# Attention with the scores made transposed: 128 keys by 512 queries, a running maximum over halves of the keys, no turning of the weights

## The reference

```python
def _L1_attn_ref(x, Wq, bq, Wk, bk, Wv, bv):
    B, S, D = (4, 4096, 256)
    q = jnp.einsum('bsd,ed->bse', x, Wq) + bq
    k = jnp.einsum('bsd,ed->bse', x, Wk) + bk
    v = jnp.einsum('bsd,ed->bse', x, Wv) + bv
    d = q.shape[-1]
    scores = jnp.einsum('bqd,bkd->bqk', q, k) / jnp.sqrt(jnp.asarray(d, q.dtype))
    w = jax.nn.softmax(scores, axis=2)
    out = jnp.einsum('bqk,bkd->bqd', w, v)
    return out
...
    t = t + _L1_attn_ref(_ln_t(t), L1_attn_Wq, L1_attn_bq, L1_attn_Wk, L1_attn_bk, L1_attn_Wv, L1_attn_bv)
```

## Time and profile before

| what | value |
|---|---|
| median of 3 runs | 4358.04 us (4357.77 to 4361.45) |
| the profiled execution's own time | 4359.66 us |
| its span, first to last instruction | 4357.9 us |
| mean granted TensorE clock | 0.966 |
| busy PE, PEld, DVE, ACT, POOL | 89, 72, 59, 54, 32% of the span |

### The profile page before, as it was taken

The page is one execution under the profiler, slowest core; times in us unless marked ns, Lnnn a source line. Parts: engine busy times, 40 slices in busy tenths (PEclk is TensorE's granted clock), DMA queues, the critical chain, the costliest instruction groups (busy, mean ns, idle before and its releaser), DMA issues. The chain is left out here.

```text
span 4357.9 us, 86111 instructions
## 1 busy us (share of the span) xinstructions
PE 3863.0 (89%) x31423; PEld 3149.2 (72%) x31423; DVE 2561.1 (59%) x3778; ACT 2334.1 (54%) x6118; POOL 1389.7 (32%) x826
## 2 busy tenths in 40 slices
PE   8874888688879979999999989999999967788897
PEld 5542666466668856888888867888888844588886
DVE  2657999799947743444444423444444434477787
ACT  3433777577735534555555534555555511277776
POOL 0446999799935521000000011000000000022254
PEclk9987999899989989999999999999999989999999
DMA  4364111411133320000000010000000033445565
GB/s 128 88 172 116 40 42 43 107 42 43 39 84 103 105 74 20 10 10 10 10 11 11 10 46 13 10 10 10 10 10 10 10 103 135 161 136 137 139 202 172
DMA packets 203913, 286.36 MB, mean 66 GB/s; under 512 B 19680, under 2 KB 157792, under 8 KB 203104
## 3 DMA queue, kind: packets, MB, share of 16 engines
q1 hardware_dynamic: 194528, 275.79, 21.6%
q10 hardware_dynamic: 9216, 8.39, 0.6%
HBM read 191.84 MB, written 92.27 MB: 65 GB/s over the span
## 5 line engine op out<-in xcount | busy, mean ns | idle before, releaser
L631 POOL TENSOR_TENSOR mp_Z<-mp_lvs,mx_rv 128x1280 f32<-128x1280 f32 (+1 forms) x256 | 796.5, 3353 | 64.0 <-ACT mp_lvs L554 39.2
L611 DVE TENSOR_TENSOR mp_Z<-mp_psL,mx_rv 128x2816 f32<-128x2816 f32 (+1 forms) x256 | 785.7, 3150 | 45.9 <-DMA mx_rv<-rv 25.3
L1195 DVE TENSOR_REDUCE sv_mx<-sv_S 128x1 f32<-128x512 f32 x512 | 351.5, 686 | 652.8 <-ACT sv_S L1164 652.8
L561 ACT ACTIVATE mp_cut<-mp_psO,mx_mask 128x128 f32<-128x128 f32 x2048 | 549.9, 403 | 157.5 <-PE mp_psO L504 157.5
L1143 PE MATMUL sv_psO<-at_v_hi,sv_p_hi 128*128 128x256 f32 x2048 | 623.1, 304 | 11.0 <-DVE sv_p_lo L1205 5.0
L504 PE MATMUL mp_psO<-mp_Z,mp_pair 128*16 128x256 f32 x8192 | 503.4, 387 | 107.3 <-POOL mp_Z L631 95.0
L1143 PE MATMUL sv_psO<-at_v_hi,sv_p_lo 128*128 128x256 f32 x2048 | 577.8, 282 | 0.0
L1143 PE MATMUL sv_psO<-at_v_lo,sv_p_hi 128*128 128x256 f32 x2048 | 577.2, 282 | 0.0
L1164 ACT COPY sv_S<-sv_psS 128x512 f32<-128x512 f32 x512 | 300.3, 586 | 511.9 <-PE sv_psS L1127 499.0
L504 PEld LDWEIGHTS mp_psO<-mp_Z,mp_pair 128*16 128x16 f32 x8192 | 339.3, 124 | 246.8 <-DVE mp_Z L611 136.0
L1114 POOL CAST sv_q_hi<-at_qT 128x256 fp32r x64 | 25.4, 397 | 1482.4 <-PE sv_psS L1127 1476.9
(11 more groups left out here) (188 smaller groups left out, 7107.9 us busy)
## 6 DMA issues: line engine op xcount, KB each, us to landing
re_xg<-xg SPq DMA_DIRECT2D x192, 384.0 KB, 3.3
xg<-ga_xg SPq DMA_DIRECT2D x32, 768.0 KB, 3.7
mp_pair<-att SPq DMA_DIRECT2D x128, 128.0 KB, 2.6
fr_xr<-in_x SPq DMA_DIRECT2D x16, 512.0 KB, 4.5
fr_xl<-in_x SPq DMA_DIRECT2D x32, 256.0 KB, 4.3
rv<-fr_rvs SPq DMA_DIRECT2D x16, 512.0 KB, 2.9
att<-mx_rv SPq DMA_DIRECT2D x16, 512.0 KB, 7.0
att<-fr_E SPq DMA_DIRECT2D x16, 512.0 KB, 6.4
```

Source lines behind the costliest of these rows:

```text
L561: ins = nc.scalar.activation(cut[:, s, c, :, h * DK:(h + 1) * DK], psO[:, c % 2, :, h * DK:(h + 1) * DK], ACT.Copy, scale=mask[:, h:h + 1])
L611: nc.vector.tensor_tensor(Z[:, c, 0:m], psL[:, s, 0:D].unsqueeze(1).broadcast_to([P, m, D]), rv[:, c * YC:c * YC + m, :], ALU.mult).then_i ...
L631: nc.gpsimd.tensor_tensor(Z[:, c, m:YC], lvs[:, s, :].unsqueeze(1).broadcast_to([P, YC - m, D]), rv[:, c * YC + m:(c + 1) * YC, :], ALU.mu ...
L1195: nc.vector.tensor_reduce(mx[:, s, c:c + 1], S[:, s, c, :], AX_X, ALU.max).then_inc(maxed, 1)
```

## The change

Scores are made the other way round: the keys are the stationary side, and a block has 128 keys on the partitions and 512 queries in the columns. A query block is 512 queries, 8 of them, each against 32 key blocks; all is written out, with one running number `u` (256 per batch). The exponents of such a block already have keys on the partitions, so `p_hi` and `p_lo` are made from `S` in SBUF, and nothing is turned.

The maximum over the keys now lies across partitions. It is taken over halves of the keys, 16 blocks each (`SC`): VectorE keeps a running maximum of whole blocks (`running_max`), TensorE turns it with four transposes (`turn`), VectorE reduces them to one number per query (`top_of`), and TensorE spreads those over the partitions into `psM` (`spread_top`). VectorE subtracts `psM` from the scores (`shift`), ScalarE takes the exponent without a bias. The first half's output is copied to `acc` (`evict`), and `finish` multiplies it by the exponent of the difference of the two tops (`fade`) and adds the second half's. The values get two more columns, ones and zeros, so that the weights' sum comes out of the weighing as column 256.

A block is weighed 18 units (`LAG`) behind its scores. `S` has 18 slots. `psS` has 2 banks instead of 4, `psO` 4. The queries no longer stay in SBUF: `qk` stores them in DRAM, `sv` loads 512 at a time, and GpSimd splits them 128x1024 at once.

```diff
+    VW = D + 2
+    q_d = nc.dram_tensor(f"q{b}", (KT, P, T), F32, kind="Internal").ap()
...
-        qT = ph.sb("qT", [P, KT, T])
...
-        v_hi = ph.sb("v_hi", [P, T // P, D], F32R)
-        v_lo = ph.sb("v_lo", [P, T // P, D], F32R)
+        v_hi = ph.sb("v_hi", [P, NT, VW], F32R)
+        v_lo = ph.sb("v_lo", [P, NT, VW], F32R)
...
-                    with sp.Fori(0, NBLK // 2) as r:
-                        for s in range(2):
-                            n = r * 2 + s
-                            sp.wait_ge(made, HEAD + (n - 1) * 6)
-                            sp.dma_start(xs[:, s], xlT_d[:, :, bass.ds(n * BLK + b * T, BLK)].rearrange("k p t -> p k t")).then_inc(x_in[s], 16)
+                    for s in range(2):
+                        load(s, s)
+                    for n in range(NBLK):
+                        s = n % 2
+                        if n + 2 < NBLK:
+                            load(n + 2, s)
+                        sp.wait_ge(q_kept, HEAD + (n + 1) * KT)
+                        sp.dma_start(q_d[:, :, n * BLK:(n + 1) * BLK].rearrange("k p t -> p k t"), qs[:, s]).then_inc(q_out[s], 16)
+                    for s in range(2):
+                        sp.wait_ge(q_out[s], HEAD + 16 * (NBLK // 2))
...
+                            act.wait_ge(q_out[s], HEAD + r * 16)
...
+                                if j < KT:
+                                    nc.scalar.activation(qs[:, s, j, :], psP[:, j, :], ACT.Identity, bias=bias[0][:, j:j + 1]).then_inc(q_kept, 1)
...
+            C = T // P
+            SC = C // 2
+            R = SC + 2
+            LAG = SC + 2
+            NU = NBLK * C
+            q = ap.sb("q", [P, KT, BLK])
+            q_hi = ap.sb("q_hi", [P, 2, KT, BLK], F32R)
+            q_lo = ap.sb("q_lo", [P, 2, KT, BLK], F32R)
+            S = ap.sb("S", [P, R, BLK])
...
+            psS = ap.ps("psS", [P, 2, BLK])
+            psX = ap.ps("psX", [P, KB, P])
+            psM = ap.ps("psM", [P, KB, P])
+            psO = ap.ps("psO", [P, KB, 512])
...
+                    def load_q(n):
+                        reach(sp, q_cut, n)
+                        sp.dma_start(q[:, :, :], q_d[:, :, n * BLK:(n + 1) * BLK].rearrange("k p t -> p k t")).then_inc(q_in, 16)
+                    load_q(0)
+                    load_q(1)
+                    for n in range(NBLK):
+                        rows = slice(n * BLK, (n + 1) * BLK)
+                        reach(sp, t2_out, n * 16)
+                        sp.dma_start(t[:, :, :], t_d[b, rows, :].rearrange("(u p) d -> p u d", p=P)).then_inc(t_in, 16)
+                        if n + 2 < NBLK:
+                            load_q(n + 2)
+                        sp.wait_ge(added, (n + 1) * KB)
+                        sp.dma_start(t2_d[b, rows, :].rearrange("(u p) d -> p u d", p=P), t[:, :, :]).then_inc(t2_out, 16)
+                    sp.wait_ge(t2_out, 16 * NBLK)
...
+                    for n in range(NBLK):
+                        pool.wait_ge(q_in, (n + 1) * 16)
+                        reach(pool, scored, (n - 1) * C)
+                        nc.gpsimd.tensor_copy(q_hi[:, n % 2], q[:, :, :]).then_inc(q_hi_cut, 1)
+                        pool.wait_ge(q_hi_cut, n + 1)
+                        pool.sem_inc(passed, 1)
+                        nc.gpsimd.tensor_tensor(q_lo[:, n % 2], q[:, :, :], q_hi[:, n % 2], ALU.subtract).then_inc(q_cut, 1)
...
+                    def score(u):
+                        n, c = u // C, u % C
+                        pe.wait_ge(q_cut, n + 1)
+                        reach(pe, kept, u - 1)
+                        terms = [(a, x, k) for k in range(KT) for a, x in ((k_hi, q_hi), (k_hi, q_lo), (k_lo, q_hi))]
+                        for i, (a, x, k) in enumerate(terms):
+                            mm = pe.matmul(psS[:, u % 2, :], a[:, k, c * P:(c + 1) * P], x[:, n % 2, k, :], start=(i == 0), stop=(i == len(terms) - 1))
...
-                    def turn(n, s, c):
-                        pe.wait_ge(exped, HEAD + n * C + c + 1)
-                        pe.wait_ge(pT_kept, HEAD + n * C + c - 1)
-                        for t in range(KB):
-                            mm = pe.transpose(psT[:, c % 2, t * P:(t + 1) * P], S[:, s, c, t * P:(t + 1) * P], ident[:, :])
...
+                    def turn(m):
+                        pe.wait_ge(maxed, (m + 1) * (SC - 1))
+                        reach(pe, topped, m)
+                        for j in range(KB):
+                            mm = pe.transpose(psX[:, j, :], run[:, m % 2, j * P:(j + 1) * P], ident[:, :])
                         mm.then_inc(turned, 1)
...
+                    def spread_top(m):
+                        pe.wait_ge(topped, m + 1)
+                        reach(pe, shifted, m * SC)
+                        for j in range(KB):
+                            mm = pe.transpose(psM[:, j, :], top[:, m % 2, j:j + 1].broadcast_to([P, P]), ident[:, :])
+                        mm.then_inc(spread, 1)
...
+                    def weigh(u):
+                        m, i, c = u // SC, u % SC, u % C
+                        pe.wait_ge(p_kept, u + 1)
+                        terms = ((p_hi, v_hi), (p_hi, v_lo), (p_lo, v_hi))
+                        for j in range(KB):
+                            if i == 0:
+                                reach(pe, evicted, (m - 1) * KB + j + 1)
+                            for e, (a, x) in enumerate(terms):
+                                mm = pe.matmul(psO[:, j, 0:VW], a[:, u % 2, j * P:(j + 1) * P], x[:, c, :],
...
+                    for u in range(NU + LAG):
+                        if u < NU:
+                            score(u)
+                        if u % SC == 0 and 0 < u <= NU:
+                            spread_top(u // SC - 1)
+                        if u >= LAG:
+                            weigh(u - LAG)
+                        if u % SC == SC - 1 and u < NU:
+                            turn(u // SC)
...
+                    def keep(u):
+                        act.wait_ge(scored, u + 1)
+                        reach(act, p_kept, u - R + 1)
+                        nc.scalar.copy(S[:, u % R, :], psS[:, u % 2, :]).then_inc(kept, 1)
+                    def exponent(u):
+                        act.wait_ge(shifted, u + 1)
+                        nc.scalar.activation(S[:, u % R, :], S[:, u % R, :], ACT.Exp, scale=SCALE).then_inc(exped, 1)
+                    def keep_hi(u):
+                        act.wait_ge(exped, u + 1)
+                        reach(act, weighed, u - 1)
+                        nc.scalar.copy(p_hi[:, u % 2], S[:, u % R, :]).then_inc(hi_kept, 1)
+                    def evict(m):
+                        act.wait_ge(weighed, (m + 1) * SC)
+                        reach(act, added, m // 2 * KB)
+                        for j in range(KB):
+                            nc.scalar.copy(acc[:, j, :], psO[:, j, 0:VW]).then_inc(evicted, 1)
+                        act.wait_ge(differed, m // 2 + 1)
+                        nc.scalar.activation(fade[:, :], fall[:, :], ACT.Exp, scale=SCALE).then_inc(faded, 1)
+                    for u in range(NU + LAG + 1):
+                        done = u - 1 - LAG
+                        if done >= 0 and done % C == SC - 1:
+                            evict(done // SC)
+                        if u < NU:
+                            keep(u)
+                        if 0 <= u - SC < NU:
+                            exponent(u - SC)
+                            keep_hi(u - SC)
...
+                    def running_max(u):
+                        m, i = u // SC, u % SC
+                        if i == 0:
...
+                            before = run[:, m % 2, :]
+                        nc.vector.tensor_tensor(run[:, m % 2, :], before, S[:, u % R, :], ALU.max).then_inc(maxed, 1)
...
+                    def shift(u):
+                        dve.wait_ge(spread, u // SC + 1)
+                        nc.vector.tensor_tensor(S[:, u % R, :], S[:, u % R, :], psM[:, :, :].rearrange("p u t -> p (u t)"), ALU.subtract).then_inc(shifted, 1)
+                    def keep_lo(u):
+                        dve.wait_ge(hi_kept, u + 1)
+                        reach(dve, weighed, u - 1)
+                        nc.vector.tensor_tensor(p_lo[:, u % 2], S[:, u % R, :], p_hi[:, u % 2], ALU.subtract).then_inc(p_kept, 1)
+                    def finish(m):
+                        n = m // 2
+                        dve.wait_ge(weighed, (m + 1) * SC)
+                        dve.wait_ge(faded, n + 1)
+                        dve.wait_ge(evicted, m * KB)
+                        for j in range(KB):
+                            nc.vector.scalar_tensor_tensor(out=acc[:, j, :], in0=acc[:, j, :], scalar=fade[:, j:j + 1], in1=psO[:, j, 0:VW],
+                                                           op0=ALU.mult, op1=ALU.add).then_inc(evicted, 1)
+                        dve.wait_ge(evicted, (m + 1) * KB)
```

(63 more changed lines are left out.)

177 lines of the change are left out of this document (53 added, 124 removed).

## The result

The changed kernel took 4188.7 us (median of 4 runs, 4178.7 to 4194.4) against 4358.4 for the kernel before (4357.8 to 4361.5): a ratio of 0.961, with the 95% interval 0.959 to 0.963. The forecast was 4191. The profiled execution took 4186.1 us, its span is 4184.3.

The account below looks back on a forecast made before the run. TensorE, busy 99% of the attention, was taken as the bound. Attention falls 94.1 us per batch, edges add 5.9 and 4.8: -83.4 per batch, -167 in all, from 4358.0 to 4191 us; range 4150 to 4235.

Parts of the forecast that it names:

- The unit: One 128 by 512 score block on TensorE: 3.25 us falls to 2.82 without its four transposes, priced at 0.43.
- 258 columns: Weighing matmuls with 258 columns instead of 256, at 0.44 ns per column: 2.7 us more per batch.
- the rival in which the rows stream at the plain f32 pace: Weighing: 258-column rows cost 0.107 us more per matmul, 657 us in all, giving 4848 us; chance 4%.
- The new transposes: TensorE, per half of the keys: four transposes of the running maximum and four spreading the tops, 13.8 us per batch.
- The stalls: TensorE's waits at turns, finishes, evictions, tops, drain and GpSimd's lock: 18.7 us per batch, against 19.2 before.
- finish of a block: VectorE's burst ending a query block delays the weights; TensorE loses 1.1 us in 7 of 8 blocks, 7.7 per batch.
- turns, with GpSimd's lock: TensorE waits for a half's last maximum: 0.2 us for 16 turns, 1.6 for the first, plus 2.2 per batch for GpSimd.
- tops: A second half's reduction and two short operations end about with the scores: 0.14 us per block, 1.1 per batch.
- eviction: ScalarE's four copies of 258 columns free the banks nearly in time: 0.15 us lost per block, 1.2 per batch.
- drain and first weighing: At a batch's end 16 weighings run alone, costing 1.6 us; 0.3 us more before the first weighing.
- The forecast holds 4.4 of them: GpSimd's passes block two-source VectorE operations: 49 us if paid in full, of which the forecast counted 4.4.
- Edges: Per batch, +5.9 us at the start for loading and splitting queries, +4.8 at the end for VectorE operations and a larger store.

Follow-up runs that it names:

- fourth-pass kernel: The changed kernel with an extra two-source VectorE maximum, result unused, ahead of each running maximum: 4246.8 us, 0.974 of the kernel before.

## Why the prediction was right

**The unit.** 2.82 us was forecast, and 2.818 and 2.825 were measured. The price of the transposes, 0.43, came from two effects in one row group (0.35 start to start, 0.08 in the matmul behind them); two kernels that put such transposes in show 0.44.

**258 columns.** 2.7 us per batch were set down for them, 0.01 per unit. The unit's 2.818 doesn't show them; the rival in which the rows stream at the plain f32 pace is gone, at 0.118 us per weighing.

**The new transposes.** 13.8 us per batch were forecast, 0.43 for each four. The timeline has 0.41 from the start of the maximum's four to the next score and 0.355 from that of the tops' four to the next weighing, and the matmul behind either group is followed 0.08 later than usual: 16 x (0.49 + 0.44) = 14.9.

**The stalls.** 18.7 and 6.0 for the rest were forecast, 24.7. Measured is 760.4 - 721.9 - 14.9 = 23.6. Since a wait of a weight load overstates the loss, the parts are read from the matmuls' starts, as here, where the tops of a second half come late:

```profile
1857.06 0.40 PE L1138 MATMUL sv_psS<-sv_q_hi,at_k_lo 128*128 128x512 f32 x1
1857.68 0.65 PE L1153 MATMUL sv_psM<-at_ident,sv_top 128*128 128x128 f32 x4 [0.22 <-DVE sv_top L1240]
1858.09 0.37 PE L1164 MATMUL sv_psO<-at_v_hi,sv_p_hi 128*128 128x258 f32 x1
1858.29 0.29 PE L1164 MATMUL sv_psO<-at_v_lo,sv_p_hi 128*128 128x258 f32 x1
```

That is 0.62 us to the first transpose and 0.41 for the four, where a first half, in which nothing waits, has 0.235 and 0.355: 0.43 lost, by the unrounded starts. In the same way, us per batch:

| term | forecast | by the starts | by the waits |
|---|---|---|---|
| finish of a block, 7 times | 7.7 | 5.7 | 7.6 |
| turns, with GpSimd's lock | 6.8 | 5.8 | 6.8 |
| tops | 1.1 | 3.9 | 5.2 |
| eviction | 1.2 | 1.3 | 1.3 |
| drain and first weighing | 1.9 | 2.1 | 2.7 |
| sum | 18.7 | 18.8 | 23.6 |

The sum is right and its parts less so, which is luck as far as they cancel. **The tops are the term that was mis-sized**: "two short operations" were taken as short beside GpSimd too, and the lock was put down to the turns only. It holds the smaller of them for 0.6 us in twelve of sixteen blocks, and a wait of 1.22 at the end of each batch, where no scores cover the tops, was not in the walk. The fourth-pass kernel, where VectorE comes later, has 2.4 us of waits for the tops, and so has the one with GpSimd later. The finish was oversized: its 1.09 us of waiting cost 0.81. The eviction is one wait at each batch's end, not 0.15 in each block. What is left beside these terms is 4.8 us, where 6.0 were carried over.

**The lock.** "The forecast holds 4.4 of them" (of the 49 us) was half of what the lock cost: moving GpSimd's passes won 9.3 us. The 4.4 were right for the turns, where the waits fell by 4.5 us; the 7.9 by which the waits for the tops fell were missing. The Trainium skill's exclusive lock ("SBUF — State Buffer", section "SBUF: two separate sides") agrees with L1240's 634 and 163 ns. The delay follows GpSimd's operation and not the size of what is held up: four columns took 0.80 us instead of 0.16.

**Edges.** The start was forecast at +5.9 per batch. The gap before the first score grew by 5.5 (7.19 against 1.65), but from the load of the identity to the first score the stretch grew by 4.75 and 5.3 in the two batches; where the difference went wasn't traced. The end was forecast at +4.8:

```profile
3327.45 1.66 DVE L1261 SCALAR_TENSOR_TENSOR sv_acc<-sv_acc,sv_fade,sv_psO 128x258 f32<-128x258 f32 x4 [1.81 <-PE sv_psO L1164]
...
3329.36 1.67 DVE L1268 SCALAR_TENSOR_TENSOR sv_t<-sv_acc,sv_rden,sv_t 128x256 f32<-128x256 f32 x4
3331.06 0.38 SPq L1117 DMA_DIRECT2D t<-sv_t  x1
```

3.9 us from the last weighing (its start is 3327.13) to the store, as walked, and the store lands after 2.9 us by the page, not 3.2. Measured are +3.6 behind batch 1; between the batches end and start together are +9.8 of 10.7.

**The sum.** -166.8 was forecast (-167 in the text), -173.6 is the difference of the two profiled executions and -170 that of the medians. Of the 6.8 us between the first two, 5.9 are the attention parts and 3.2 the edges; 2.4 the other way lie ahead of the attention. The median of the changed kernel itself came out as 4188.7 and 4181.9 in two measurements, so the 2 us between 4188.7 and the forecast say no more than that the sum is right to within some 10 us.

## What to carry to other kernels

When one engine is busy 98% of a stage, price a unit of its order from start to start, the matmul behind the removed ones included: transposes between matmuls cost more than their own starts show. Then walk the other engines' orders for the places where bursts stand (the finish of a block, the turn of a half), because slack that is ample per unit runs out there, and a burst spread over four units was worth 13 us. Price a stall by the starts of the matmuls around it: a weight load can wait in nearly every unit (413 of 512) and cost 0.03 us in most of them. And look for small operations with two SBUF sources beside long GpSimd ones, by their mean against another of their size.
